# Second layer norm of a fused attention and MLP kernel: squares moved from ScalarE to VectorE, and two tiles normalised at a time

## The reference

```
x  = layernorm(x + attention(x))      # chunked linear attention, 8 heads of 128
x  = layernorm(x + ffn(x))            # the part that this change touches

ffn(x): h = gelu(x @ fq(W_fc).T + b_fc + 2 * lora)          # 1024 -> 4096
        y = h @ fq(W_proj).T + b_proj + 2 * lora            # 4096 -> 1024
layernorm(x): m = mean(x); v = var(x); (x - m) / sqrt(v + 1e-5)
fq(W): rounded to a grid of 255 steps, scale = max|W| / 127
```

## Time and profile before

| | |
|---|---|
| median of three runs | 4352.77 us |
| the profiled execution, its time | 4351.55 us |
| its span (slowest core, core 5) | 4349.9 us (cores: 4336.1 to 4349.9) |
| TensorE, matmul busy | 3386.6 us, 78% |
| ScalarE busy | 1590.7 us, 37% |
| VectorE busy | 1339.9 us, 31% |
| GpSimd busy | 131.9 us, 3% |
| mean granted TensorE clock | 0.866 (pass 2 from 2414 us on: 0.94) |

### The profile page before, as it was taken

How to read it: one execution, slowest core, us unless ns; L and a number is a source line. 1 busy time by engine, 2 the same in 40 slices (tenths; PEclk the granted TensorE clock), 3 DMA queues, 4 the chain that set the end, 5 groups by cost and what they waited for, 6 DMA issues and landing times.

```text
span 4349.9 us, 61567 instructions; the slowest of 8 cores (4336.1 to 4349.9 us)
## 1 busy us (share of the span) xinstructions
PE 3386.6 (78%) x21768; PEld 2034.2 (47%) x21768; DVE 1339.9 (31%) x1970; ACT 1590.7 (37%) x2641; POOL 131.9 (3%) x217
## 2 busy tenths in 40 slices
PE   0877777777777777334489898998989899898997
PEld 0444444444444444201155565555656555565554
DVE  0344444444444444378821111111111111101111
ACT  0233333333333333388833333333333333333332
POOL 0000000000000000000000000000000000000000
PEclk9988888888888888655589999999999999999998
DMA  6222222222222222133300001010010100101000
GB/s 116 49 68 68 69 68 68 68 69 68 68 68 69 68 71 66 68 111 104 103 27 33 30 30 40 20 40 30 30 39 20 39 30 30 39 21 40 30 30 20
DMA packets 77971, 231.30 MB, mean 53 GB/s; under 512 B 7760, under 2 KB 24400, under 8 KB 77664
## 3 DMA queue, kind: packets, MB, share of 16 engines
q1 hardware_dynamic: 36368, 134.80, 9.5%
q0 software_dynamic: 41312, 92.55, 8.0%
HBM read 185.65 MB, written 67.11 MB: 58 GB/s over the span
## 4 chain that ended last, share of the span: by engine, by line
PE 66%; ACT 13%; DVE 11%; issue 6%; DMA 4%; ACTq 0%; DVEq 0%; POOL 0%; SPq 0%; POOLq 0%
PE pH L937 20%; PE pA L919 11%; PE pB L919 10%; PE pR L275 5%; PE pOA L401 4%; PE pOB L401 3%; PE pR L298 3%; PE pD L275 2%; PE pD L298 2%; DVE osq L360 2%; ACT x_fm L901 2%; ACT out L833 2%; PE pR L595 1%; DVE rowsA L325 1%; DVE k_sb L284 1%
## 5 line engine op out<-in xcount | busy, mean ns | idle before, releaser
L937 PE MATMUL pH<-WpjT,h 128*128 128x512 bf16 x4096 | 1118.7, 399 | 117.4 <-ACT h L926 117.4
L919 PE MATMUL pA<-x_fm,WfcT 128*128 128x256 bf16 x4096 | 582.7, 290 | 94.0 <-ACT x_fm L901 94.0
L937 PEld LDWEIGHTS pH<-WpjT,h 128*128 128x128 bf16 x4096 | 413.0, 102 | 436.1 <-issue 184.0
L919 PE MATMUL pB<-x_fm,WfcT 128*128 128x256 bf16 x4096 | 562.9, 283 | 0.0
L919 PEld LDWEIGHTS pA<-x_fm,WfcT 128*128 128x128 bf16 x4096 | 422.2, 104 | 288.2 <-issue 136.8
L988 DVE TENSOR_TENSOR r<-pH,x1tm 128x512 f32<-128x512 f32 x128 | 88.6, 692 | 1368.6 <-PE pH L977 1358.3
L926 ACT ACTIVATE h<-pA,bfc_sb 128x256 bf16<-128x256 f32 x512 | 242.6, 474 | 695.7 <-PE pA L919 694.4
L919 PEld LDWEIGHTS pB<-x_fm,WfcT 128*128 128x128 bf16 x4096 | 413.4, 101 | 168.8 <-issue 10.8
L926 ACT ACTIVATE h<-pB,bfc_sb 128x256 bf16<-128x256 f32 x512 | 242.7, 474 | 606.1 <-PE pB L919 602.3
L275 PE MATMUL pR<-x_fm,WqT 128*128 128x512 bf16 x768 | 188.6, 402 | 106.4 <-DMA x_fm<-xT 106.1
L595 PE MATMUL pR<-v_sb,ktm_sb 128*128 128x128 bf16 x512 | 61.6, 295 | 228.4 <-DVE state_sb L584 136.7
(11 more groups left out here) (166 smaller groups left out, 3897.3 us busy)
## 6 DMA issues: line engine op xcount, KB each, us to landing
x_tm<-x SPq DMA_DIRECT2D x16, 2048.0 KB, 9.4
x1s<-x1o POOLq DMA_DIRECT2D x64, 512.0 KB, 3.9
x1tm<-x1s SPq DMA_DIRECT2D x32, 1024.0 KB, 4.8
y<-out POOLq DMA_DIRECT2D x64, 512.0 KB, 3.2
wst_sb<-wfcT SPq DMA_DIRECT2D x32, 512.0 KB, 4.1
x_fm<-xT POOLq DMA_DIRECT2D x16, 1024.0 KB, 10.6
wst_sb<-wprojT SPq DMA_DIRECT2D x32, 512.0 KB, 3.9
wstg<-wfcT SPq DMA_DIRECT2D x32, 512.0 KB, 4.1
```

The costliest lines, as they stand in the source:

```text
L919: e.matmul(p[:, 0:T2], WfcT[:, d_ * FF + f_ * 128:d_ * FF + f_ * 128 + 128], x1_fm[:, d_ * T2:(d_ + 1) * T2], start=(d_ == 0), stop=(d_ == ...
L937: e.matmul(pH[ii * 2 + hf][:], h1_sb[bb][:, ii * 128:ii * 128 + 128], WpjT[:, f_ * D + hf * 512:f_ * D + hf * 512 + 512], start=(f_ == 0), ...
```

## The change

```diff
@@ emit_ln2
-            P.wait("scalar", res_t[-1])
-            P.wait("scalar", res_t[-2])
-            P.wait("scalar", fr2["out"])
+            P.wait("vector", res_t[-1])
+            P.wait("vector", res_t[-2])
+            P.wait("vector", fr2["out"])
             sqs = []
             for i2 in range(2):
-                sqs.append(P.op("scalar", "ac", lambda e, ii=i2, bb=b: e.activation(
-                    out_sb[0][:], r2_sb[bb][:, ii * D:(ii + 1) * D], AF.Square,
-                    accum_out=R1(2 + ii)[:])))
+                sqs.append(P.op("vector", "ve", lambda e, ii=i2, bb=b:
+                           e.scalar_tensor_tensor(
+                               out_sb[0][:], r2_sb[bb][:, ii * D:(ii + 1) * D],
+                               1.0, r2_sb[bb][:, ii * D:(ii + 1) * D],
+                               OP.mult, OP.mult, accum_out=R1(2 + ii)[:])))
@@ the loop over fc
-                if fc == 4 and pending_ln2:
-                    pending_ln2.pop(0)()
+                if fc == 4 and t % 2 == 0:
+                    while pending_ln2:
+                        pending_ln2.pop(0)()
```

## The result

The changed kernel takes 4469.7 us (median of eight runs, 4468.5 to 4477.0) against 4352.8 for the kernel before: a ratio of 1.027, 95% interval 1.0259 to 1.0282, or 117 us more. The prediction was 4473 us, range 4445 to 4505.

What follows compares the result with a forecast made beforehand. Pass 2 was taken as bound by TensorE, standing still where ScalarE's GELU is late. Stalls removed -171.4, even-tile stalls +274.5, end +17.8 gave +120.9 us on 4351.55: 4472, stated as 4473 us, range 4445 to 4505.

Steps and rivals of the forecast that it cites:

- What a layer norm costs TensorE: Pass 2, second matmuls, tiles 1 to 31: 5.53 us per layer norm, 3.68 idle and 1.85 of slower matmuls; 171 us in all.
- Odd tiles lose nothing: Tiles 1 to 31, odd: nothing left on ScalarE between GELU(3) and GELU(4), so 16 x 5.53 = 88.5 us gained.
- The first layer norm of a pair is hidden: Even tiles: VectorE's squares and variance end at 3037.6, 2.4 us before ScalarE comes to the root.
- The second root waits for ten operations and two stores: Even tiles, ScalarE: about 14.6 us waiting for the variance, GELU(4) queued behind; TensorE idle 15.8 us instead of 3.68.
- The rival with the squares not waiting: Even tiles, second pair of squares on VectorE starts 1.3 us earlier, without waiting for the store: 4453 us; chance 5%.
- The clock behind the stall: Even tiles, TensorE after the long idle: 2.5 us lost to the low clock, between 1.85 and 3.9.
- Behind the last tile: End of the kernel, last adds to last multiply: two layer norms on the path, 30.5 us, 17.8 more than before.
- Sum: Whole kernel: -171.4 + 274.5 + 17.8 = +120.9 us on the profiled 4351.55, so 4472, stated as 4473.
- grouping the roots wins: Even tiles: both roots run one behind the other on ScalarE, h2 1.4 us late; 4219 us, 3% faster; chance 3%.

Runs made afterwards that it cites:

- three neighbouring kernels: Against the changed kernel: no store wait between the roots, 4408 us; only the dump moved, 4464, 4468 and 4479 us; squares left on ScalarE, 4519 us.
- the experiment: Against the kernel before: two layer norms in even tiles, with row sums, squares and variances on VectorE right behind each tile's adds; 4207 us, ratio 0.965.

## Why the prediction was right

- *What a layer norm costs TensorE.* 5.53 us was read in one tile; the median over the tiles is 5.52, and 3.68 us idle in each. Right.
- *Odd tiles lose nothing.* Right: TensorE waits for GELU 15 times for long, not 31.
- *The first layer norm of a pair is hidden.* Right, with 2.5 us to spare.
- *The second root waits for ten operations and two stores.* 14.6 us forecast, 14.53 the median; idle 15.8 forecast, 15.64 the median. One tile is out of the pattern: in tile 2 the second store was waited for 4.06 us instead of 1.3 to 1.6, and the stall was 18.5 us. Why wasn't looked into. The rival with the squares not waiting is refuted: the wait is in the list and in the trace.
- *The clock behind the stall.* 2.5 us forecast between bounds of 1.85 and 3.9 (behind the short stall the clock was low for 3.4 us, near the "about 3.5" of the forecast, of which the earlier trace rows shows 2); 18.03 - 15.64 = 2.4 measured. The size was right but partly by luck: the forecast had 2.5 "nearer to the first, because the matmuls here are without pauses", and in three neighbouring kernels with the same matmuls behind the stall it was 3.0 (below).
- *Behind the last tile.* The last adds end at 4436.22 and the last multiply at 4466.32, 30.1 us; 30.5 forecast, 12.65 before.

```profile
4433.14 3.08 DVE L991 TENSOR_TENSOR r<-pH,x1tm 128x512 f32<-128x512 f32 x4 [60.07 <-PE pH L980]
4465.57 0.75 DVE L860 TENSOR_SCALAR out<-out,rows 128x1024 f32<-128x1024 f32 x1
```

- *Sum.* Odd tiles 16 x 5.52 = 88 less; 14 even tiles 18.03 - 5.52 = 12.5 more each, 175; tile 2 some 16 more; behind the last tile 17.5 more: 120. Measured 117. The 3 us between are the size of the boundaries: a pair of tiles grew by 6.81 us on average (136.54 to 143.35, tiles 4 to 30), while the stalls account for 7.0. So the total is near the forecast by a little luck too: tile 2's 3 us too many and the boundaries' 3 us too few cancel.
- *The rival "grouping the roots wins"*, 3%, was wrong for this kernel and right as a mechanism: it put a pair with ready roots at 1.4 us lost, and the experiment gave 1.36. The Trainium skill's rule of finishing one table set before switching (ScalarE: Activation LUTs, "Rules for kernel authors") paid here only where both inputs existed. It was worth little even then: 4207 us against 4222 with a root in each tile.

The expectations for the experiments missed by up to 18 us (4468 for 4450, where only the dump moved). The idle times were within 0.2 us each time. In the three kernels with long stalls 7 to 9 us of the miss lie in the clock's return (0.5 to 0.6 us more than taken, 15 times), and some at the tile boundaries; the rest is open. Even within one execution the eight cores of the changed kernel come to tile 1 between 2203 and 2223 us.

## What to carry to other kernels

Before two operations are grouped on an engine that works in list order, look at what the second one needs: if another engine makes its input from a chain that begins with the first one's result, everything queued behind waits for the whole chain, here 14.5 us to save 2.6 us of table loads. Price an engine's help to a bottleneck by what stands between two of its urgent operations, not by its busy share: VectorE at 31% and ScalarE at 37% both had room, and still the kernel took 4207 or 4470 us by where the row sums, squares and variances stood in VectorE's list. Best of all was to leave nothing of it on ScalarE, the engine that TensorE waits for: 15 tiny operations per tile on VectorE in place of one and the root, and the kernel at 4189 us, 3.8% under the one before.

## What was not expected of the hardware

How long TensorE runs at 1.2 GHz behind a stall does not follow the length of the stall. Median idle time over the tiles of one profile each, and what the median loss is beyond it:

```
idle us   0.81   1.2    3.68   10.9   14.46   15.64   17.83
more us   0.16   0.16   1.84   3.07   2.99    2.39    3.00
```

Up to 1.2 us idle the clock stayed at 1.00. At 3.68 us it fell only after the matmuls had resumed, and was low for 3.4 us. From 10.9 us on it was already at 0.50 at the resumption. On the slowest cores it came back 4.1 to 4.8 us later in the changed kernel (15.64), and 5.4 to 6.0 in the others, tile 2 apart. So the longest idle time but one has the shortest return. The other seven cores give the same further loss within 0.1 us by the median, so this goes with the kernel and not with the core. Nor is it the length alone within a kernel: in tile 2 of the one without waits for stores the idle time is 10.90 us as in most of its tiles, but the further loss is 1.5 us on four cores, 1.9 on one and 3.0 on the other three. When the stall falls may matter beside how long it is; no run tests that. A change that takes 1.2 us out of each stall can come out at nothing, as that of the dump did. A forecast of such a kernel has, as an estimate from these figures, ±0.6 us per stall and about ±0.25 us per tile boundary, 10 to 20 us in all.
